# Decoder layer kernel: three elementwise sums moved from GpSimd to VectorE, and two one-column steps written as a tensor with two scalars

## The chip, the cores and the metric

One core of one Trainium2 chip runs the kernel. The metric is the device time of one execution in microseconds (us). A core has TensorE (PE: matmuls and transposes, with its weight loads PEld), VectorE (DVE), ScalarE (ACT), GpSimd (POOL) and SyncE (SP, which here only issues transfers). Each engine has a program of its own, in order, and they meet at semaphores.

## The reference, cut to what matters

One pre-norm decoder layer over 32 sequences of 128 tokens by 512 features: self attention, cross attention to a context of 128 tokens, and a mixture of 64 experts of which every token takes 8.

```python
def _layernorm(x, axis=-1, eps=1e-05):
    m = jnp.mean(x, axis=axis, keepdims=True)
    v = jnp.var(x, axis=axis, keepdims=True)
    return (x - m) / jnp.sqrt(v + eps)
...
    x = x + _L0_attn_ref(_layernorm(x, axis=-1), L0_attn_Wq, L0_attn_bq, L0_attn_Wk, L0_attn_bk, L0_attn_Wv, L0_attn_bv, L0_attn_Wo, L0_attn_bo)
    x = x + _L0_xattn_ref(_layernorm(x, axis=-1), ctx_2048, L0_xattn_wq, L0_xattn_bq, L0_xattn_wkv, L0_xattn_bkv, L0_xattn_wp, L0_xattn_bp)
    x = x + _L0_ffn_ref(_layernorm(x, axis=-1), L0_ffn_router_w, L0_ffn_w_gate, L0_ffn_w_up, L0_ffn_w_down)
    return x
```

Keys and values of the cross attention are projections of the context in full precision. Queries and output of the cross attention are quantised to 8 bits and back.

## The kernel before, in words

A tile is one sequence, 128 tokens on the 128 partitions. The first phase (to about 1240 us) is a software pipeline: in iteration `cur` the engines work at once on five tiles, `cur - 1` (its first layer norm), `cur - 2` (projection of queries and keys), `cur - 3` (self attention, context keys), `cur - 4` (cross attention) and `cur - 5` (second sum, third layer norm, router, scatter of the normed rows to the experts' places in DRAM). There is one `body(cur)` for each engine, a list written out by hand that fixes the order of that engine's steps. Iterations 7 to 32 are a hardware loop, those before and after it are written out. The second phase goes through the 64 experts.

A full-precision projection is made of matmuls on a high part and a low part. For the context, `ctx_hi` (L1747) rounds the loaded `ctx_sb` to `cT_hi`, and `ctx_lo` (L1756) makes the rest, `cT_lo = ctx_sb - cT_hi`. TensorE reads both for the keys (`cross_keys_a`, `cross_keys_c`, `cross_keys_b`) and in the next iteration for the values (`cross_values_b`, `_a`, `_c`).

`bias_residual` (L1768) adds the output bias of the self attention to the residual input `x_res`, which `first_sum` (L1362) adds to the projection one iteration later. `bias_first_sum` (L1775) adds the cross attention's output bias to `x1` and leaves it in `x1_bias` for `second_sum` (L1317, L1320), one iteration later. `ctx_lo`, `bias_residual` and `bias_first_sum` are GpSimd's here, beside `ctx_hi`, the power -1/2 of the three layer norms (`rsqrt`, L1741), `number_tokens` (L1763) and the scatter (L1786, eight indirect DMAs a tile).

The layer norms (kinds "self", "cross", "ffn") go from VectorE (`norm_start`: L1242, L1245, L1247) to GpSimd (`rsqrt`) and back (`norm_scale`: L1252, L1255, L1257, one Newton step on one column). `ffn_shifted` (L1454) makes the shift that ScalarE needs for `ffn_normed` (L1082).

VectorE's part of `body` around the change, in its order (line of the instruction): `cross_max_0`, `cross_max_1` (L1276), `copy_cross_values` (L1437), `ffn_rsqrt` (L1252, L1255, L1257), `ffn_shifted` (L1454), `self_statistics` (L1242, L1245, L1247), `max_3`, `max_1`, `max_2`, `max_0` (L1276), `self_rsqrt`, `norm_probs_3`, `norm_probs_2` (L1282, L1285), `copy_cross_keys` (L1480), `norm_probs_1`. ScalarE's exponentials `exp_3`, `exp_2` and so on (L985) wait for the maxima and are waited for by `norm_probs_3` and `norm_probs_2`. TensorE's `turn_probs_3` (L533) comes right after `logits` (L555) in its order and waits for `copy_cross_keys`:

```python
            def turn_probs_3(m):
                reached(pe, e_xk, m, 1, 1)
                turn_probs(1, 3, p_pT)
```

`until` is a semaphore wait, and `reached` waits for the value that step j of tile m leaves.

Of the kernel before, what the change touches and what calls it, by code (L numbers as in the profile page):

```python
# [38 lines left out]
B = 32  # L39
# [66 lines left out]
def layer(nc, x, ctxT_in, qT_w, kT_w, vT_w, oT_w, xkT_w, xvT_w, xq_w, xp_w, biases, vb, xkb, xvb, ob, xbq, xbp, routerT,  # L106
# [10 lines left out]
    with st:  # L117
# [167 lines left out]
        g_cT = sem("pool_ctxT")  # L285
        g_x1b, g_tok = sem("pool_x1_bias"), sem("pool_token_number")
        g_res = sem("pool_residual_bias")
# [63 lines left out]
        def _(sp):  # L351
# [48 lines left out]
            def load_context(m):  # L400
                reached(sp, g_cT, m - 1, 2, 2)
                sp.dma_start(ctx_sb[:, :].rearrange("p (t n) -> p t n", t=KT),
                             ctxT_in[tile(m)].rearrange("(t p) n -> p t n", p=P)).then_inc(s_ctx, 16)
# [37 lines left out]
            for cur in range(B + 1, B + 6):  # L441
                body(cur)
                if cur == B + 3:
                    for projected in (p_q, p_k, p_v, p_xk, p_o):
                        sp.wait_ge(projected, 3 * B)
                    for k in range(2):
                        load_weights(k, k)
                if cur == B + 4:
                    for k in range(2, 8):
                        load_weights(k, k)  # L450
                    sp.wait_ge(p_xv, 3 * B)
                    for k in range(8, 10):
                        load_weights(k, k)
                    sp.wait_ge(p_xpv, 4 * B)
                    sp.wait_ge(g_res, B)
                    for k in range(10, 14):
                        load_weights(k, k)
# [28 lines left out]
        def _(pe):  # L486
# [151 lines left out]
            def cross_keys_a(m):  # L638
                reached(pe, g_cT, m, 2, 1)
# [12 lines left out]
            def cross_keys_c(m):  # L652
                reached(pe, g_cT, m, 2, 2)
                project(1, cT_hi, cT_lo, "xk", 2, False, False).then_inc(p_xk, 1)
# [583 lines left out]
        def _(dve):  # L1238
# [10 lines left out]
            def norm_scale(kind, m):  # L1249

                s, c = d_ln[kind], ln[kind]
                dve.scalar_tensor_tensor(out=c["t"], in0=c["v"], scalar=c["r0"], in1=c["r0"], op0=ALU.mult,  # L1252
                                         op1=ALU.mult).then_inc(s, 1)
# [105 lines left out]
            def first_sum(m):  # L1359
                reached(dve, p_o, m, 3, 3)  # L1360
                reached(dve, g_x1b, m - 1, 1, 1)
# [39 lines left out]
            def second_sum(m):  # L1401
# [3 lines left out]
                if isinstance(m, int):  # L1405
                    reached(dve, g_x1b, m, 1, 1)
# [32 lines left out]

            def ffn_rsqrt(m):  # L1440
# [11 lines left out]
            def ffn_shifted(m):  # L1452
                reached(dve, d_ln["ffn"], m, 7, 6)
                dve.scalar_tensor_tensor(out=ffn_shift, in0=ln["ffn"]["mv"][:, 0:1], scalar=-1.0, in1=ln["ffn"]["r"],  # L1454
                                         op0=ALU.mult, op1=ALU.mult).then_inc(d_ln["ffn"], 1)
# [75 lines left out]
            def body(cur):  # L1531
# [36 lines left out]
                if has(cur - 4):  # L1568
                    copy_cross_values(cur - 4)
                if has(cur - 5):  # L1570
# [3 lines left out]
                if has(cur - 1):  # L1574
                    self_statistics(cur - 1)
                if has(cur - 3):
# [161 lines left out]
        def _(pool):  # L1738
# [14 lines left out]
            def ctx_lo(m):  # L1753
                reached(pool, g_cT, m, 2, 1)
                reached(pool, p_xv, m - 1, 3, 3)
                pool.tensor_tensor(flat(cT_lo), ctx_sb[:, :], flat(cT_hi).bitcast(F32), ALU.subtract).then_inc(g_cT, 1)  # L1756

# [8 lines left out]
            def bias_residual(m):  # L1766
                reached(pool, s_x_res, m, 16, 16)
                pool.tensor_tensor(x_res[:, :], x_res[:, :], att_bias[:, :], ALU.add).then_inc(g_res, 1)  # L1768

# [3 lines left out]

            def bias_first_sum(m):
                pool.tensor_tensor(x1_bias, x1[:, :], xp_bias[:, :], ALU.add).then_inc(g_x1b, 1)  # L1775
# [14 lines left out]
            def body(cur):  # L1790
# [4 lines left out]
                if has(cur - 3):  # L1795
                    ctx_lo(cur - 3)
                if has(cur - 5):
                    number_tokens(cur - 5)
                if has(cur - 3):
                    bias_residual(cur - 3)  # L1800
                if has(cur - 1):
                    self_power(cur - 1)
                if has(cur - 4):
                    bias_first_sum(cur - 4)
# [113 lines left out]
```

## Time and profile before

| | |
|---|---|
| median of 3 runs | 1647.8 us (1643.46 to 1648.24) |
| the profiled execution | 1644.18 us, of which the span is 1642.4 us |
| mean granted TensorE clock | 0.972 |
| busy share of the span | PE 92%, PEld 71%, DVE 74%, ACT 52%, POOL 42% |
| first phase / second phase | to about 1240 us / 1240 to 1642 us |

Rows of the timeline begin with the start in us from the span's first instruction and the duration in us. "[0.64 <-DVE ...]" is the engine's idle time just before the row and the instruction that ended it. Two VectorE instructions that do not depend on each other overlap by some 0.08 us, so the spacing of their starts is less than the duration. One iteration of the pipeline takes 35.6 us.

### The profile page before, as it was taken

To read this page: it belongs to the slowest core of one execution; us is meant where nothing else is said; L and a number is where in the kernel's file an instruction comes from. 1 tells how busy PE (TensorE), PEld (TensorE's weight loads), DVE (VectorE), ACT (ScalarE), POOL (GpSimd) and SP (SyncE) were. 2 spreads that over 40 slices of the span, in tenths; PEclk is the share of its full clock that TensorE was granted. 3 is DMA by queue.
4 is the path that set the end of the run, shared out by engine and by line. 5 is a ranking of instruction groups with operands and counts; after the bars stand their busy time and mean duration, and the time that the engine had idled before them with its cause. 6 is when DMAs were issued, how large, how long until landed. Compare 5 with 4: busy or idle time off the path is not lost.

```text
span 1642.4 us, 34879 instructions
## 1 busy us (share of the span) xinstructions
PE 1515.1 (92%) x11025; PEld 1158.6 (71%) x11058; DVE 1222.1 (74%) x3203; ACT 853.8 (52%) x2737; POOL 682.9 (42%) x656
## 2 busy tenths in 40 slices
PE   2799999999999999999999999999888888888895
PEld 1577778777778777777877787887645655556563
DVE  6578888889888888888888888888842444444453
ACT  3356666555666655666665566665532333333342
POOL 0013443344443334444334444433443445455465
PEclk9799999999999999999999999999999999999998
DMA  9752322222111101111001011010196999999964
GB/s 323 282 221 84 110 95 89 88 101 107 65 44 30 26 27 31 26 38 32 26 26 32 26 38 32 26 27 21 42 372 207 275 273 275 269 270 284 279 97 51
DMA packets 159883, 195.68 MB, mean 119 GB/s; under 512 B 39686, under 2 KB 122118, under 8 KB 159825
## 3 DMA queue, kind: packets, MB, share of 16 engines
q1 hardware_dynamic: 120912, 157.14, 29.2%
q0 software_dynamic: 38912, 37.87, 11.2%
q8 instruction: 24, 0.39, 0.1%
q14 instruction: 35, 0.28, 0.1%
HBM read 127.47 MB, written 130.29 MB: 157 GB/s over the span
## 4 chain that ended last, share of the span: by engine, by line
PE 61%; DMA 20%; issue 8%; POOL 3%; DVE 1%; ACT 1%; POOLq 0%; SPq 0%; DVEq 0%; ACTq 0%
PE bank L508 30%; DMA out<-x,slots 19%; PE bank L533 7%; PE bank L541 6%; PE bank L490 5%; PE bank L526 4%; PE bank L514 3%; PE bank L549 2%; PE bank L555 2%; PE bank L521 1%; POOL routed L1786 1%; PE bank L495 1%; PE bank L925 0%; ACT probs L985 0%; POOL small L1741 0%
## 5 line engine op out<-in xcount | busy, mean ns | idle before, releaser
L985 ACT ACTIVATE probs<-bank,small 128x128 f32<-128x128 f32 x1024 | 328.0, 417 | 46.0 <-DVE small L1276 46.0
L1786 POOL DMA_INDIRECT routed<-row,slots x248 | 258.7, 1043 | 77.6 <-issue 71.3
L1741 POOL TENSOR_TENSOR small<-small,half 128x1 f32<-128x1 f32 x96 | 62.1, 646 | 540.2 <-DVE small L1247 540.2
L1856 POOL DMA_INDIRECT out<-x,slots x128 | 200.9, 1569 | 197.5 <-DMA out<-x,slots 144.2
L979 ACT ACTIVATE probsT<-bank 128x512 f32<-128x512 f32 x256 | 163.2, 653 | 27.3 <-PE bank L533 27.3
L1276 DVE TENSOR_REDUCE small<-bank 128x4 f32<-128x512 f32 x256 | 161.5, 683 | 12.8 <-PE bank L526 11.6
L533 PE MATMUL bank<-idf,probs 128*128 128x128 f32 x1024 | 154.7, 279 | 3.2 <-DVE xk_sb L1480 2.4
L979 ACT ACTIVATE xo8T<-bank 128x512 bf16<-128x512 bf16 x32 | 19.1, 597 | 241.4 <-PE bank L495 241.4
L1696 DVE TENSOR_SCALAR slots<-pairs 128x1 uint32<-128x1 f32 x128 | 13.7, 149 | 174.0 <-DMA out<-x,slots 170.5
L533 PEld LDWEIGHTS bank<-idf,probs 128*128 128x128 f32 x1024 | 118.7, 143 | 28.7 <-issue 6.1
L985 ACT ACTIVATION_READ_ACCUMULATOR probs<-bank,small 128x1 f32 x512 | 131.7, 257 | 0.0
L541 PE MATMUL bank<-xv,probsT 128*128 128x33 f32 x1024 | 119.8, 272 | 0.0
L541 PEld LDWEIGHTS bank<-xv,probsT 128*128 128x128 f32 x1024 | 119.4, 192 | 0.0
L1205 ACT ACTIVATE xn<-bank 128x192 f32<-128x192 f32 x64 | 21.2, 331 | 153.8 <-PE bank L925 153.8
L925 PE MATMUL bank<-w_gate_up,x_res 128*128 128x384 f32 x256 | 98.9, 535 | 0.0
L925 PE MATMUL bank<-w_gate_up,x_in 128*128 128x384 f32 x256 | 96.3, 523 | 0.6 <-issue 0.6
L1285 DVE TENSOR_TENSOR probs<-probs,small 128x512 f32<-128x512 f32 x128 | 88.6, 693 | 4.4
L925 PEld LDWEIGHTS bank<-w_gate_up,x_res 128*128 128x128 f32 x256 | 51.0, 210 | 30.0 <-issue 8.2
L925 PEld LDWEIGHTS bank<-w_gate_up,x_in 128*128 128x128 f32 x256 | 49.7, 204 | 30.3 <-issue 7.3
L508 PE MATMUL bank<-w_q_hi,xT_hi 128*128 128x512 f32 x128 | 54.7, 427 | 17.4 <-POOL bias_of L1832 17.4
L1747 POOL CAST cT_hi<-ctx_sb 128x512 fp32r<-128x512 f32 x32 | 19.6, 613 | 105.4 <-PE bank L508 57.6
L1024 ACT ACTIVATE wide_b<-bank,xq_bs,xq_ws 128x128 f32<-128x128 f32 x128 | 48.1, 456 | 23.9 <-PE bank L490 23.9
(244 smaller groups left out, 4000.0 us busy)
## 6 DMA issues: line engine op xcount, KB each, us to landing
w_gate_up<-in_w_gate SPq DMA_DIRECT2D x128, 192.0 KB, 3.7
w_gate_up<-in_w_up SPq DMA_DIRECT2D x128, 192.0 KB, 3.9
w_down<-in_w_down SPq DMA_DIRECT2D x128, 192.0 KB, 4.4
routed<-empty_row SPq DMA_DIRECT2D x4, 5120.0 KB, 19.6
x_in<-in_x SPq DMA_DIRECT2D x32, 256.0 KB, 3.1
ctx_sb<-in_ctxT_in SPq DMA_DIRECT2D x32, 256.0 KB, 2.8
x_res<-in_x SPq DMA_DIRECT2D x32, 256.0 KB
out<-x SPq DMA_DIRECT2D x32, 256.0 KB, 2.1
```

What stands on the lines that cost most here:

```text
L490: last = pe.transpose(bank[:, b, t * P:(t + 1) * P], src[:, t * P:(t + 1) * P], idf[:, :])
L508: done = pe.matmul(bank[:, b, :], lhsT, rhs, start=first and k == 0, stop=last and k == len(steps) - 1)
L526: last = pe.matmul(bank[:, b, i * P:(i + 1) * P], q[own, i, :], keys[own, i, :], start=not masked, stop=not masked or i == NG - 1)
L533: last = pe.transpose(bank[:, b, j * P:(j + 1) * P], probs[:, g, j * P:(j + 1) * P], idf[:, :])
L541: last = pe.matmul(bank[:, b, at:at + VW], probsT[:, g, i * P:(i + 1) * P], vals[:, h, :], start=True, stop=True)
L925: last = pe.matmul(bank[:, 2 + k % 2, 0:2 * F], rowsT[k % 2][:, t * P:(t + 1) * P], w_gu[k][:, :, t, :], start=(t == 0), stop=(t == KT - 1))
L979: act.activation(dst, src, ACT.Copy).then_inc(done, 1)
L985: last = act.activation(probs[:, g, j * P:(j + 1) * P], bank[:, b, j * P:(j + 1) * P], ACT.Exp, bias=negated[:, h:h + 1], **({"accum_out": ...
L1276: dve.tensor_reduce(negated[:, g * GH:(g + 1) * GH], bank[:, b, :].rearrange("p (j k) -> p j k", j=GH), AX_X, ALU.max, negate=True).then_i ...
L1285: dve.tensor_tensor(heads, heads, own.unsqueeze(2).to_broadcast([P, GH, P]), ALU.mult).then_inc(d_norm, 1)
L1786: pool.indirect_dma_start(routed, bass.IndirectOffsetOnAxis(ap=slots_of(m)[:, k:k + 1], axis=0), row_of(m)[:, :], None, bounds_check=SLOTS ...
L1856: pool.indirect_dma_start(out.rearrange("b p (h c) -> (b p h) c", h=2), bass.IndirectOffsetOnAxis(ap=place_of[k % 2][:, half_:half_ + 1], ...
```

## The change

`ctx_lo`, `bias_residual` and `bias_first_sum` become VectorE's, at three places of its order: `ctx_lo` behind `copy_cross_values`, `bias_residual` and `bias_first_sum` between `self_statistics` and `max_3`. Semaphores follow: `first_sum` waits for one more. The first step of `norm_scale` and `ffn_shifted`, each a scalar_tensor_tensor on one column, become tensor_scalar with two scalars.

```diff
@@ norm_scale
-                dve.scalar_tensor_tensor(out=c["t"], in0=c["v"], scalar=c["r0"], in1=c["r0"], op0=ALU.mult,
-                                         op1=ALU.mult).then_inc(s, 1)
+                dve.tensor_scalar(c["t"], c["v"], c["r0"], c["r0"], ALU.mult, ALU.mult).then_inc(s, 1)
@@ load_context (SP), cross_keys_a, cross_keys_c (PE)
-                reached(sp, g_cT, m - 1, 2, 2)
+                reached(sp, d_cT, m - 1, 1, 1)
...
-                reached(pe, g_cT, m, 2, 1)
+                reached(pe, g_cT, m, 1, 1)
...
-                reached(pe, g_cT, m, 2, 2)
+                reached(pe, d_cT, m, 1, 1)
@@ first_sum
-                reached(dve, g_x1b, m - 1, 1, 1)
+                reached(dve, d_x1b, m - 1, 1, 1)
+                reached(dve, d_res, m, 1, 1)
@@ VectorE, new steps
+            def ctx_lo(m):
+                reached(dve, g_cT, m, 1, 1)
+                dve.tensor_tensor(flat(cT_lo), ctx_sb[:, :], flat(cT_hi).bitcast(F32), ALU.subtract).then_inc(d_cT, 1)
+
+            def bias_residual(m):
+                reached(dve, s_x_res, m, 16, 16)
+                dve.tensor_tensor(x_res[:, :], x_res[:, :], att_bias[:, :], ALU.add).then_inc(d_res, 1)
+
+            def bias_first_sum(m):
+                dve.tensor_tensor(x1_bias, x1[:, :], xp_bias[:, :], ALU.add).then_inc(d_x1b, 1)
@@ ffn_shifted
-                dve.scalar_tensor_tensor(out=ffn_shift, in0=ln["ffn"]["mv"][:, 0:1], scalar=-1.0, in1=ln["ffn"]["r"],
-                                         op0=ALU.mult, op1=ALU.mult).then_inc(d_ln["ffn"], 1)
+                dve.tensor_scalar(ffn_shift, ln["ffn"]["mv"][:, 0:1], ln["ffn"]["r"], -1.0, ALU.mult,
+                                  ALU.mult).then_inc(d_ln["ffn"], 1)
@@ VectorE's body
                 if has(cur - 4):
                     copy_cross_values(cur - 4)
+                if has(cur - 3):
+                    ctx_lo(cur - 3)
...
                 if has(cur - 1):
                     self_statistics(cur - 1)
+                if has(cur - 3):
+                    bias_residual(cur - 3)
+                if has(cur - 4):
+                    bias_first_sum(cur - 4)
                 if has(cur - 3):
                     max_3(cur - 3)
@@ GpSimd's body: the three steps are gone
```

## Rows read from the trace of the kernel before

**Rows 1.** One stretch: its length, then busy us of PE, PEld, DVE, ACT, POOL:
```profile
600.00:635.60 35.60, 35.46 (x288) 28.27 (x289) 31.65 (x83) 21.88 (x77) 15.02 (x17) 1.00 0.10 30
```

**Rows 2.** Timeline of DVE, from the cross values' copy to the first maximum:
```profile
629.66 0.68 DVE L1437 TENSOR_TENSOR xv<-bank,xv_bias 128x512 f32<-128x512 f32 x1
630.26 0.91 DVE L1252 SCALAR_TENSOR_TENSOR small<-small 128x1 f32<-128x1 f32 x1
...
631.58 1.19 DVE L1454 SCALAR_TENSOR_TENSOR small<-small 128x1 f32<-128x1 f32 x1
632.69 0.68 DVE L1242 BATCH_NORM_STATS2 small<-x_in 128x6 f32<-128x512 f32 x1
...
633.79 2.48 DVE L1276 TENSOR_REDUCE small<-bank 128x4 f32<-128x512 f32 x4
```

**Rows 3.** Timeline of POOL, same stretch:
```profile
629.88 1.26 POOL L1756 TENSOR_TENSOR cT_lo<-ctx_sb,cT_hi 128x512 fp32r<-128x512 f32 x1
...
631.49 1.26 POOL L1768 TENSOR_TENSOR x_res<-x_res,att_bias 128x512 f32<-128x512 f32 x1
633.93 0.57 POOL L1741 TENSOR_TENSOR small<-small,half 128x1 f32<-128x1 f32 x1 [1.18 <-DVE small L1247]
```

**Rows 4.** Timeline of ACT, the start of the self attention's exponentials:
```profile
634.52 0.37 ACT L985 ACTIVATE probs<-bank,small 128x128 f32<-128x128 f32 x1 [0.64 <-DVE small L1276]
```

**Rows 5.** Timeline of DVE, `norm_probs_2` and `copy_cross_keys` (35.6 us before: same place):
```profile
602.33 0.18 DVE L1282 RECIPROCAL small<-small 128x4 f32<-128x4 f32 x1 [0.30 <-ACT probs L985]
602.54 0.69 DVE L1285 TENSOR_TENSOR probs<-probs,small 128x512 f32<-128x512 f32 x1
603.15 0.68 DVE L1480 COPY xk_sb<-bank 128x512 f32<-128x512 f32 x1
```

**Rows 6.** Timeline of PE, around `turn_probs_3`, mid-loop:
```profile
602.90 1.08 PE L555 MATMUL bank<-router_w,x3T 128*128 128x64 f32 x8
603.89 1.09 PE L533 MATMUL bank<-idf,probs 128*128 128x128 f32 x8
```

**Rows 7.** Timeline of PE, the same place in iteration 35:
```profile
1175.06 1.08 PE L555 MATMUL bank<-router_w,x3T 128*128 128x64 f32 x8
1175.98 1.04 PE L533 MATMUL bank<-idf,probs 128*128 128x128 f32 x8
```

**Rows 8.** Timeline of DVE, the iteration of one late scatter:
```profile
665.24 0.68 DVE L1437 TENSOR_TENSOR xv<-bank,xv_bias 128x512 f32<-128x512 f32 x1
...
667.74 1.39 DVE L1257 TENSOR_TENSOR small<-small 128x1 f32<-128x1 f32 x1
...
670.38 2.48 DVE L1276 TENSOR_REDUCE small<-bank 128x4 f32<-128x512 f32 x4
```

**Rows 9.** Timeline of PE, `turn_probs_3` two iterations after that of rows 6:
```profile
676.08 1.09 PE L533 MATMUL bank<-idf,probs 128*128 128x128 f32 x8
```

**Rows 10.** Timeline of DVE, iteration 35:
```profile
1164.26 0.69 DVE L1437 TENSOR_TENSOR xv<-bank,xv_bias 128x512 f32<-128x512 f32 x1 [0.29 <-PE bank L508]
...
1169.58 2.48 DVE L1276 TENSOR_REDUCE small<-bank 128x4 f32<-128x512 f32 x4
```

**Rows 11.** Groups of DVE's instructions by line (busy us, mean ns | idle before):
```profile
L1262 DVE TENSOR_SCALAR xn<-x_in,small 128x512 f32<-128x512 f32 x32 | 17.2, 538 | 0.1
L1371 DVE TENSOR_SCALAR xo_tmp<-xatt,small 128x512 f32<-128x512 f32 x32 | 15.3, 479 | 0.0
L1334 DVE TENSOR_SCALAR small<-small 128x1 f32<-128x1 f32 x32 | 6.9, 215 | 1.1
```

**Rows 12.** Timeline of DVE, the first two iterations of self attention:
```profile
60.82 2.09 DVE L1313 TENSOR_TENSOR roped<-roped,wide_a 128x1024 f32<-128x1024 f32 x1
...
99.79 2.48 DVE L1276 TENSOR_REDUCE small<-bank 128x4 f32<-128x512 f32 x4 [0.67 <-PE bank L526]
```

**Rows 13.** Timeline of DVE and then POOL, during the cross norm's power:
```profile
615.88 0.43 DVE L1375 TENSOR_SCALAR xo<-xo_tmp 128x512 bf16<-128x512 f32 x1
...
615.53 0.82 POOL L1741 TENSOR_TENSOR small<-small,half 128x1 f32<-128x1 f32 x1 [15.38 <-DVE small L1247]
```

More of the change, by code:

```diff
@@ L284, in layer @@
         g_pow = {k: sem(f"pool_rsqrt_{k}") for k in ln}
-        g_cT = sem("pool_ctxT")
-        g_x1b, g_tok = sem("pool_x1_bias"), sem("pool_token_number")
-        g_res = sem("pool_residual_bias")
+        g_cT, d_cT = sem("pool_ctxT_hi"), sem("dve_ctxT_lo")
+        g_tok = sem("pool_token_number")
+        d_x1b, d_res = sem("dve_x1_bias"), sem("dve_residual_bias")
         s_vspread, s_att = sem("value_bias_spread"), sem("attention_bias")
@@ L454, in _ @@
                     sp.wait_ge(p_xpv, 4 * B)
-                    sp.wait_ge(g_res, B)
+                    sp.wait_ge(d_res, B)
                     for k in range(10, 14):
@@ L1405, in second_sum @@
                 if isinstance(m, int):
-                    reached(dve, g_x1b, m, 1, 1)
+                    reached(dve, d_x1b, m, 1, 1)
                 second_sum_of(6, m)
@@ L1751, in ffn_power @@
                 rsqrt("ffn")
[L1753 to L1756, printed above, removed]
             def number_tokens(m):
@@ L1764, in number_tokens @@
                                    ALU.add).then_inc(g_tok, 1)
-            def bias_residual(m):
-                reached(pool, s_x_res, m, 16, 16)
-                pool.tensor_tensor(x_res[:, :], x_res[:, :], att_bias[:, :], ALU.add).then_inc(g_res, 1)
             def self_power(m):
@@ L1772, in self_power @@
                 rsqrt("self")
-            def bias_first_sum(m):
-                pool.tensor_tensor(x1_bias, x1[:, :], xp_bias[:, :], ALU.add).then_inc(g_x1b, 1)
             def cross_power(m):
@@ L1794, in body @@
                     ffn_power(cur - 5)
-                if has(cur - 3):
-                    ctx_lo(cur - 3)
                 if has(cur - 5):
                     number_tokens(cur - 5)
-                if has(cur - 3):
-                    bias_residual(cur - 3)
                 if has(cur - 1):
                     self_power(cur - 1)
-                if has(cur - 4):
-                    bias_first_sum(cur - 4)
                 if has(cur - 3):
```

## The prediction

> **What bounds the kernel now.** I read the stretches view first, then the timelines of the engines over one iteration, then the waits. In a mid-loop iteration of 35.60 us TensorE is busy for 35.46, VectorE for 31.65 and GpSimd for 15.02 [rows 1]. That looks like a kernel bound by TensorE, in which VectorE has 4 us to spare. A busy TensorE can still be held for less than the overlap of its instructions, so I followed who hands work to whom.
>
> Follow one chain. `copy_cross_values` starts at 629.66, and from there VectorE works without a wait up to `max_3` at 633.79, which is 4.13 us later [rows 2]. ScalarE has idled for 0.64 us until that maximum ends, and starts the exponentials at 634.52 [rows 4]. It then works through its list at its own pace; the reader sees in the same place one iteration earlier that VectorE's `norm_probs_2` idles 0.30 us for it, and that `copy_cross_keys` follows and ends at 603.15 + 0.68 = 603.83 [rows 5]. TensorE's `turn_probs_3`, which needs this copy, starts at 603.89 [rows 6]. So the last link is 0.06 us wide. In iteration 35, where nothing holds it there, `turn_probs_3` starts 0.92 us after `logits`; mid-loop it is 0.99 [rows 6, 7]. TensorE is held for 0.07 us an iteration by a chain that runs through VectorE's stretch of 4.13 us. Idle time of VectorE elsewhere is no help: it lies behind waits for ScalarE.
>
> The trace holds its own test of this. Once, GpSimd's scatter is late, and VectorE's stretch lasts 670.38 - 665.24 = 5.14 us, 1.01 more [rows 8]. `turn_probs_3` then starts at 676.08, 72.19 us after 603.89, which is two iterations of 35.60 and 0.99 more [rows 6, 9]. A microsecond in this stretch is a microsecond of the kernel. The change edits exactly this stretch.
>
> **The change, part by part.** Removed, stalls: in the stretch VectorE's two one-column scalar_tensor_tensor wait behind GpSimd. L1252 starts at 630.26 and ends at 631.17, L1756 of GpSimd ends at 631.14; L1454 starts at 631.58 and ends at 632.77, L1768 ends at 632.75 [rows 2, 3]. Both GpSimd instructions leave, so the stalls do.
>
> What the two instructions cost without a stall is not in the trace in their new form. A one-column tensor_scalar with one scalar from memory and one constant takes 0.215 us; a second scalar from memory adds 0.538 - 0.479 = 0.06 on 512 columns [rows 11]. So the first becomes 0.27, plus 0.03 to the dependent next one: 0.30. Bounds: 0.24, if the second scalar is free, and 0.36, if it costs twice that. It was 0.91 + 0.03 = 0.94. The shift becomes 0.215, and the independent next one overlaps it by 0.08: 0.13, where it was 632.69 - 631.58 = 1.11 [rows 2]. Removed: 0.64 + 0.98 = 1.62 us a tile.
>
> Added: three tensor_tensor of 512 columns with both inputs in SBUF. The one in rows 5 takes 0.69 and the next starts 603.15 - 602.54 = 0.61 after it. All three are independent of their neighbours: 1.83 us a tile, each in the stretch. They wait for nothing: `cT_hi` is ready ahead of 629.88, since GpSimd makes it before L1756 [rows 3], and `ctx_lo` would start at 630.26. `x_res` is loaded half an iteration before. `load_context` on SP now waits for an end at about 630.95 in place of 631.14 [rows 3], nothing is behind it that is urgent.
>
> Sum of the stretch: 4.13 - 1.62 + 1.83 = 4.34 us, so +0.21 a tile, between +0.15 and +0.27. What is late next is ScalarE's `exp_3`, then `norm_probs_2`, `copy_cross_keys` and TensorE, all by the same 0.21, as in the late iteration. The stretch is filled like this in iterations 6 to 33; 27 of them are regular: 27 x 0.21 = +5.7 us.
>
> One iteration has the late scatter: 5.14 becomes 4.34, since the freed GpSimd is no longer in the way: -0.8. Iteration 35 has a second one, 1169.58 - 1164.26 = 5.32 us [rows 10]. It has no `self_statistics` any more, which takes 633.79 - 632.69 = 1.10 [rows 2], so it becomes 4.34 - 1.10 = 3.24: -2.1, of which I take -2.0.
>
> The start: at 60.82 the rotation of the first tile takes 2.09 behind GpSimd [rows 12]. With 512 columns at 0.69 [rows 5] 1024 take at most 1.38, so at least 0.7 goes: I take -0.8. In the next iteration there is no stalled instruction to relieve, and the three additions meet an idle time of 0.67 [rows 12]: 1.83 - 0.67 = +1.16. Together +0.36.
>
> Two small ones have no row. `first_sum` gets a third wait, for a value long reached, and the cross norm's step gets the second scalar, both on the way from the output projection to `turn_quantised_x`. At nothing they cost 0, at 0.06 a tile over 31 tiles 1.9 us; I take 0.5, since TensorE's order has some play there. The self norm's step grows too, under the 0.30 us that VectorE waits for ScalarE [rows 5]; without that cover it would be another 0.06 a tile, 1.6 us. The second phase has none of the moved work: 0.
>
> Sum: 5.7 - 0.8 - 2.0 + 0.4 + 0.5 = +3.8 us. The profiled execution becomes 1644.18 + 3.8 = 1648.0. The median shown is 3.6 us above that execution, so the median becomes 1647.8 + 3.8 = **1651.6 us** (+0.23%).
>
> **The rivals.** *A. The stretch grows by 0.21* (forecast): 1651.6, by its bounds and 1 us for the start 1649 to 1655.
>
> *B. A new stall behind the power.* After `self_statistics` GpSimd starts the self norm's power, 0.57 us [rows 3], while VectorE runs `bias_residual` and then wants `bias_first_sum`. If the power gets in between and keeps VectorE out, it costs up to 0.57 a tile: 27 x 0.57 = 15.4, so 1667.0. For it: a tensor_tensor of VectorE does stall behind GpSimd, L1257 took 1.39 [rows 8]. Against it: the cross norm's power is stretched to 0.82 by VectorE's tensor_scalars, and the tensor_scalar L1375 that starts within it at 615.88 takes a plain 0.43 [rows 13]; a power seems to hold VectorE off for next to nothing. It decides only if the power takes the port in the gap and holds it over 0.04 us.
>
> The Trainium skill, "SBUF — State Buffer", section "Who interferes with whom", says of exactly these pairs that a VectorE instruction with two SBUF inputs and a GpSimd instruction that reads SBUF share a port pair, which whoever issues first keeps for its whole instruction. By that rule the power would hold off `bias_first_sum` for its whole 0.57 us, and the sum would be B's. On the long GpSimd instructions the trace agrees (0.91 and 1.19 us where the stalls end with them, [rows 2, 3]); on the power the row speaks against it [rows 13].
>
> *C. The stretch is not the bound after all.* If ScalarE or TensorE has play that the rows don't show, the 0.21 vanish and only gains stay: -0.8 at the start, -1.0 and -2.0 at the late scatters, 1647.8 - 3.8 = 1644.0. For it: TensorE is held for 0.07 us only. Against it: the 0.99 of rows 9.
>
> *D. The chain gets shorter*, the one on the faster side: if the three additions cost under 0.5 each where they stand, the stretch shrinks by more than 0.07, TensorE is no longer held, and 27 x 0.07 = 1.9 come on top of C's: 1642.1. Against it: the 0.61 between starts in rows 5, on the same form of instruction.
>
> *E. More late scatters in plain runs.* Each is worth 1.0 to the change. The runs lie 4.8 us apart; four more would give 1647.6, nine more would be needed for a clear gain.
>
> *F. The cross norm's way is as tight* as the other and its two small costs come to 0.1 a tile: 31 x 0.1 = 3.1 in place of 0.5, 1654.2.
>
> **How the numbers follow.** Chances: A 0.55, B 0.12, C 0.13, D 0.08, E 0.05, F 0.07. A measurement of this kernel tells about 0.3% from no change, 4.9 us: faster below 1642.9, slower above 1652.7. A lies 1.1 us under that line, so of its 0.55 I put 0.33 within and 0.22 above. Slower: 0.22 + 0.12 + 0.07 = 0.41. Faster: D and some of E, 0.10. Within: 0.49. The range leaves out B and most of D: from a little under C, 1643, to 1658, which takes in F and a B of a third of its price. A's own is 1649 to 1655.
>
> **What would show it.** In the changed profile: the first step of the ffn norm at about 0.27 us and the shift at 0.21, neither stalled (if stalled, something else of GpSimd reads there); `ctx_lo`, `bias_residual`, `bias_first_sum` at 0.69 each (over 0.75 for the last is B); from `copy_cross_values` to `max_3` 4.34 us (4.1 or less is D); starts of `turn_probs_3` 35.8 us apart (35.6 with a stretch of 4.34 is C); no iteration of 36.6. The prediction is wrong if the two rewritten steps cost far more than 0.3, if waits for reached values cost time on VectorE, or if the end of iteration 35 does not carry through to the second phase.

## The result and the profile after

The changed kernel takes 1649.18 us against 1643.62 us for the kernel before (medians of 17 runs each); the ratio is 1.0031, with an interval from 1.0019 to 1.0044. One execution of the changed kernel, 17% longer at a lower clock, is left out of the ratio. The profiled execution of after took 1648.34 us with a span of 1646.5 us, against 1644.18 and 1642.4 before.

The first table of the page of after, busy us, share of the span and instructions of each engine:

```profile
PE 1515.3 (92%) x11025; PEld 1157.2 (70%) x11058; DVE 1230.3 (75%) x3299; ACT 854.5 (52%) x2737; POOL 574.9 (35%) x560
```

GpSimd has 108 us less to do, VectorE 8 us more, and TensorE the same. The stretch of one mid-loop iteration, to be held against [rows 1]:

```profile
600.00:635.83 35.83, 35.69 (x289) 28.29 (x289) 31.92 (x85) 21.90 (x76) 11.71 (x13) 1.00 0.09 29
```

The iteration is 35.83 us long, 0.23 more. The timeline of VectorE from the cross values' copy to the first maximum, which answers to [rows 2]:

```profile
637.35 0.68 DVE L1437 TENSOR_TENSOR xv<-bank,xv_bias 128x512 f32<-128x512 f32 x1
637.95 0.68 DVE L1442 TENSOR_TENSOR cT_lo<-ctx_sb,cT_hi 128x512 fp32r<-128x512 f32 x1
638.54 0.27 DVE L1252 TENSOR_SCALAR small<-small 128x1 f32<-128x1 f32 x1
...
639.23 0.21 DVE L1465 TENSOR_SCALAR small<-small 128x1 f32<-128x1 f32 x1
639.36 0.68 DVE L1242 BATCH_NORM_STATS2 small<-x_in 128x6 f32<-128x512 f32 x1
...
640.47 0.69 DVE L1446 TENSOR_TENSOR x_res<-x_res,att_bias 128x512 f32<-128x512 f32 x1
641.08 0.69 DVE L1449 TENSOR_TENSOR wide_a<-x,xp_bias 128x512 f32<-128x512 f32 x1
641.68 2.48 DVE L1275 TENSOR_REDUCE small<-bank 128x4 f32<-128x512 f32 x4
```

The stretch is 641.68 - 637.35 = 4.33 us, where 4.34 was forecast. The two rewritten steps take 0.27 and 0.21, the step behind each of the three additions starts 0.59 to 0.61 later, and nothing is stalled. TensorE from the step ahead of `logits` to `turn_probs_3`, which answers to [rows 6]:

```profile
608.68 1.87 PE L541 MATMUL bank<-xv,probsT 128*128 128x33 f32 x16
610.52 1.10 PE L555 MATMUL bank<-router_w,x3T 128*128 128x64 f32 x8
611.57 1.09 PE L533 MATMUL bank<-idf,probs 128*128 128x128 f32 x8
```

It starts 1.05 us after `logits`; before it was 0.99, and 0.92 where nothing holds it [rows 6, 7]. That is only 0.06 of the 0.23. More of it lies one step earlier. `logits` itself starts 610.52 - 608.68 = 1.84 us after the step ahead of it, where it was 602.90 - 601.19 = 1.71:

```profile
601.19 1.87 PE L541 MATMUL bank<-xv,probsT 128*128 128x33 f32 x16
```

`logits` needs `x3T`, which ScalarE makes (L979). Here are the timelines of ScalarE, before and then after:

```profile
637.75 0.64 ACT L979 ACTIVATE x3T<-bank 128x512 f32<-128x512 f32 x1
...
645.63 0.64 ACT L979 ACTIVATE x3T<-bank 128x512 f32<-128x512 f32 x1
```

In both kernels this comes 3.23 us after the first exponential (634.52 before, 642.40 after), so a later maximum makes `x3T` later by the same amount. A third part, 0.03, stands at `turn_quantised_x`, which starts 0.68 us after the step ahead of it in place of 0.65. Together that is 0.06 + 0.13 + 0.03 = 0.22 of the 0.23.

**Where the time went.** The stores of x2 mark the end of each tile's attention. In the timelines of SyncE they come as follows. The first is at 126.32 before and at 130.66 after (+4.34). From there to the last but one, at 1193.17 and 1201.03, it is another +3.52. From that store to the end of the span it is 449.2 and 445.5 (-3.8). The very last store is no such mark, since it stands in SyncE's order behind the loads of the second phase's weights, as in after:

```profile
1237.17 0.91 SPq L345 DMA_DIRECT2D w_down<-in_w_down  x2
1238.12 0.44 SPq L393 DMA_DIRECT2D out<-x  x1
```

The part behind the last but one store varies from 445 to 459 us among before, after and experiments 1 to 4 and 6 to 8, whose code for the second phase is the same, so it says nothing of the change. Two parts are left: a loss of 4.3 us in the first 130 us, and one of 3.5 us in the loop. Together they are 7.9 us in these two executions, where the medians of all executions differ by 5.6; what makes up the difference between the two isn't shown.

The loop's part goes as forecast. The intervals between stores grow from 35.60 to 35.83. The one with the late scatter was 36.58 and is 35.84 (-0.74; forecast -0.8). The one that holds iteration 35 goes from 33.60 to 31.65 (-1.95; forecast -2.0), and TensorE's timeline carries this gain to the last tile: its step at 1222.81 before (L490) comes at 1230.66 after, 7.85 later, as it is at iteration 35. The other 28 intervals gain 3.52 + 0.74 + 1.95 = 6.2 us, where 5.7 + 0.5 were forecast.

The start's part does not. The stretches view of TensorE's clock shows it (columns as in [rows 1]; the third from the right is the granted clock). Before:

```profile
100.00:105.00 5.00, 5.00 (x36) 4.37 (x33) 4.29 (x12) 4.74 (x25) 1.66 (x2) 1.00 1.01 388
105.00:110.00 5.00, 4.88 (x49) 4.40 (x49) 3.88 (x11) 4.00 (x17) 0.00 (x0) 1.00 1.03 403
```

After:

```profile
100.00:105.00 5.00, 4.46 (x33) 3.95 (x30) 4.58 (x12) 4.59 (x25) 0.00 (x0) 1.00 1.02 395
105.00:110.00 5.00, 4.61 (x23) 4.61 (x23) 2.91 (x8) 3.16 (x13) 0.00 (x0) 0.54 1.03 396
110.00:115.00 5.00, 5.00 (x43) 3.88 (x47) 0.63 (x2) 2.15 (x6) 0.00 (x0) 0.50 0.66 251
```

In the second iteration of self attention TensorE is busy for 4.46 of 5 us where it was busy for 5.00, and then its granted clock goes from 1.00 (2.4 GHz) to 0.50 (1.2 GHz) for some 10 us. The timeline of TensorE shows one `turn_probs` in that time at nearly twice its length, behind `copy_cross_keys`. Before and after:

```profile
105.73 1.09 PE L533 MATMUL bank<-idf,probs 128*128 128x128 f32 x8
...
105.39 1.97 PE L533 MATMUL bank<-idf,probs 128*128 128x128 f32 x8 [0.93 <-DVE xk_sb L1491]
```

Up to here after was not late at all, but 0.34 us early. The whole loss of 4.3 us in the first store comes behind this step, with the clock down.

### The profile page after: what moved, and what is told of

Read it like the earlier page. It is cut to its first block, busy times and chain, and to the rows that moved or that the text cites. A ratio compares the mean times of both kernels' runs of the same rounds, so it can differ in the third digit from the quotient of the medians.

```text
span 1646.5 us, 34797 instructions
## 1 busy us (share of the span) xinstructions
PE 1515.3 (92%) x11025; PEld 1157.2 (70%) x11058; DVE 1230.3 (75%) x3299; ACT 854.5 (52%) x2737; POOL 574.9 (35%) x560
## 4 chain that ended last, share of the span: by engine, by line
PE 64%; DMA 19%; issue 7%; DVE 2%; POOL 1%; ACT 1%; POOLq 0%; SPq 0%; DVEq 0%
PE bank L508 31%; DMA out<-x,slots 19%; PE bank L533 7%; PE bank L541 6%; PE bank L490 5%; PE bank L526 4%; PE bank L514 3%; PE bank L549 2%; PE bank L555 2%; PE bank L521 1%; PE bank L495 1%; POOL routed L1791 1%; ACT probs L985 0%; PE bank L925 0%; DVE small L1275 0%
## 5 line engine op out<-in xcount | busy, mean ns | idle before, releaser
L1758 POOL TENSOR_TENSOR small<-small,half 128x1 f32<-128x1 f32 x96 | 74.4, 775 | 652.8 <-DVE small L1247 652.8
L979 ACT ACTIVATE probsT<-bank 128x512 f32<-128x512 f32 x256 | 162.9, 652 | 29.7 <-PE bank L533 29.5
L533 PE MATMUL bank<-idf,probs 128*128 128x128 f32 x1024 | 156.1, 281 | 4.1 <-DVE xk_sb L1491 3.4
L979 ACT ACTIVATE xo8T<-bank 128x512 bf16<-128x512 bf16 x32 | 19.1, 597 | 241.6 <-PE bank L495 241.6
L533 PEld LDWEIGHTS bank<-idf,probs 128*128 128x128 f32 x1024 | 119.7, 144 | 30.6 <-issue 6.3
L925 PE MATMUL bank<-w_gate_up,x_res 128*128 128x384 f32 x256 | 94.4, 515 | 0.0
L925 PE MATMUL bank<-w_gate_up,x_in 128*128 128x384 f32 x256 | 91.9, 504 | 0.5 <-issue 0.5
L1024 ACT ACTIVATE wide_b<-bank,xq_bs,xq_ws 128x128 f32<-128x128 f32 x128 | 48.1, 457 | 23.9 <-PE bank L490 23.9
L508 PE MATMUL bank<-w_o_hi,attT_hi 128*128 128x512 f32 x132 | 56.0, 424 | 1.7 <-issue 0.9
```

The source lines that it names most:

```text
L508: done = pe.matmul(bank[:, b, :], lhsT, rhs, start=first and k == 0, stop=last and k == len(steps) - 1)
L533: last = pe.transpose(bank[:, b, j * P:(j + 1) * P], probs[:, g, j * P:(j + 1) * P], idf[:, :])
L925: last = pe.matmul(bank[:, 2 + k % 2, 0:2 * F], rowsT[k % 2][:, t * P:(t + 1) * P], w_gu[k][:, :, t, :], start=(t == 0), stop=(t == KT - 1))
L979: act.activation(dst, src, ACT.Copy).then_inc(done, 1)
L1758: pool.tensor_tensor(c["r0"], c["v"], half[:, :], ALU.pow).then_inc(g_pow[kind], 1)
```

## The experiments

Each is read against runs of the kernel before that were made together with it. "Stretch" is the time from `copy_cross_values` to `max_3`, and "period" the usual time between two stores of x2.

**1. The two bias steps out of the stretch.** In after, the same instructions at a place where VectorE has waited for ScalarE:

```diff
-                if has(cur - 3):
-                    bias_residual(cur - 3)
-                if has(cur - 4):
-                    bias_first_sum(cur - 4)
                 if has(cur - 3):
                     max_3(cur - 3)
...
+                if has(cur - 3):
+                    bias_residual(cur - 3)
+                if has(cur - 4):
+                    bias_first_sum(cur - 4)
                 if has(cur - 3):
                     att_lo(cur - 3)
```

> The changed kernel, with bias_residual and bias_first_sum moved out of VectorE's stretch between copy_cross_values and max_3 and placed right ahead of att_lo, where VectorE idles 0.93 us for ScalarE. Same work, same engine, another place. Theory 1 (the length of the stretch sets the period, a tile for a tile): stretch 4.33 - 2 x 0.61 = 3.1 us, turn_probs_3 no longer held, period 35.5 to 35.6 in place of 35.83, so about 27 x 0.3 = 7 us less than the changed kernel, ratio to the kernel before 0.996 to 0.999. Theory 2 (VectorE's added load of 1.8 us a tile costs wherever it stands, for instance through the port it shares with GpSimd): period stays at 35.8, ratio 1.003. Theory 3 (the 4 us later start in the profile of the changed kernel come from a fall of TensorE's clock at 105 to 116 us, brought on by the longer hold in the second iteration): the hold at turn_probs_3 there shrinks from 0.93 to near nothing, and the clock stays at 1.0 there.

Measured: 1640.6 us, ratio to before 0.9958 (0.9945 to 0.9971). The timeline of VectorE of this kernel gives a stretch of 3.11 us:

```profile
627.68 0.68 DVE L1437 TENSOR_TENSOR xv<-bank,xv_bias 128x512 f32<-128x512 f32 x1
...
630.79 2.48 DVE L1275 TENSOR_REDUCE small<-bank 128x4 f32<-128x512 f32 x4
```

and that of TensorE shows `turn_probs_3` no longer held, 0.92 us behind `logits`:

```profile
636.52 1.08 PE L555 MATMUL bank<-router_w,x3T 128*128 128x64 f32 x8
637.44 1.04 PE L533 MATMUL bank<-idf,probs 128*128 128x128 f32 x8
```

The period is 35.52, the first store comes at 125.37, and the clock from 100 to 115 us is 1.00. The work is the same as in after, and only its place differs: the loss of after is that of the stretch, not of VectorE's busy time. With the longer stretch gone, `logits` is free too: it starts 1.70 us after the step ahead of it.

**2. The old forms with the moved work.** After, with both tensor_scalar back as scalar_tensor_tensor:

```diff
-                dve.tensor_scalar(c["t"], c["v"], c["r0"], c["r0"], ALU.mult, ALU.mult).then_inc(s, 1)
+                dve.scalar_tensor_tensor(out=c["t"], in0=c["v"], scalar=c["r0"], in1=c["r0"], op0=ALU.mult,
+                                         op1=ALU.mult).then_inc(s, 1)
...
-                dve.tensor_scalar(ffn_shift, ln["ffn"]["mv"][:, 0:1], ln["ffn"]["r"], -1.0, ALU.mult,
-                                  ALU.mult).then_inc(d_ln["ffn"], 1)
+                dve.scalar_tensor_tensor(out=ffn_shift, in0=ln["ffn"]["mv"][:, 0:1], scalar=-1.0, in1=ln["ffn"]["r"],
+                                         op0=ALU.mult, op1=ALU.mult).then_inc(d_ln["ffn"], 1)
```

> The changed kernel with its two one-column tensor_scalar turned back to scalar_tensor_tensor (the three sums stay on VectorE). Theory 1: no long GpSimd instruction is left in the stretch, so they do not stall any more in either form, and the old form is shorter (0.21 against 0.27, 0.16 against 0.21): stretch 4.33 - 0.11 = 4.22, period 35.72, 3 us less than the changed kernel, ratio to before about 1.001. Theory 2 (the new form is what took the stalls away): L1252 of the ffn norm and the shift stall again, at 0.4 us or more, behind the power or number_tokens, and the period is 36.0 or more, ratio 1.006.

Measured: 1649.62 us, ratio 1.0020 (1.0007 to 1.0032). The timeline of VectorE:

```profile
637.57 0.21 DVE L1252 SCALAR_TENSOR_TENSOR small<-small 128x1 f32<-128x1 f32 x1
...
638.20 0.16 DVE L1466 SCALAR_TENSOR_TENSOR small<-small 128x1 f32<-128x1 f32 x1
```

With GpSimd's long instructions gone the old forms don't stall, and they are shorter than the new ones: 0.21 against 0.27, and 0.16 against 0.21. The stretch is 4.26, the period 35.77, and the clock falls at the start as in after (first store 130.38). So the two halves of the change are two cures for one stall, and whoever moves the work away has no use for the new forms. (The ratios of this kernel and of after, 1.0020 and 1.0031, are too close to tell apart; the 0.06 us of the period are read from the traces.)

**3. The new forms alone.** Before, with only those lines changed the other way round; GpSimd keeps its three steps.

```diff
-                dve.scalar_tensor_tensor(out=c["t"], in0=c["v"], scalar=c["r0"], in1=c["r0"], op0=ALU.mult,
-                                         op1=ALU.mult).then_inc(s, 1)
+                dve.tensor_scalar(c["t"], c["v"], c["r0"], c["r0"], ALU.mult, ALU.mult).then_inc(s, 1)
...
-                dve.scalar_tensor_tensor(out=ffn_shift, in0=ln["ffn"]["mv"][:, 0:1], scalar=-1.0, in1=ln["ffn"]["r"],
-                                         op0=ALU.mult, op1=ALU.mult).then_inc(d_ln["ffn"], 1)
+                dve.tensor_scalar(ffn_shift, ln["ffn"]["mv"][:, 0:1], ln["ffn"]["r"], -1.0, ALU.mult,
+                                  ALU.mult).then_inc(d_ln["ffn"], 1)
```

> The kernel before with only the two one-column steps turned to tensor_scalar; the three sums stay on GpSimd. Theory 1 (scalars from memory do not come through the port shared with GpSimd): neither step stalls, 0.27 and 0.21 us in place of 0.91 and 1.19; the one-column tensor_tensor between them may stall by some 0.4 us until ctx_lo of GpSimd ends. Stretch 2.7 to 2.9 us in place of 4.13, turn_probs_3 not held, no late iteration: period 35.5, ratio 0.996 to 0.998. Theory 2 (the stall moves on to the next instruction of VectorE that needs the port, and all of it stays): stretch near 4.1, period 35.6, ratio 1.000. Theory 3 (the tensor_scalar stalls like the old form): the same numbers as before plus 0.1 a tile.

Measured: 1640.75 us, ratio 0.9964 (0.9952 to 0.9977). The timeline of VectorE (here L1257 of before is L1256):

```profile
628.88 0.26 DVE L1252 TENSOR_SCALAR small<-small 128x1 f32<-128x1 f32 x1
629.18 0.15 DVE L1254 TENSOR_SCALAR small<-small 128x1 f32<-128x1 f32 x1
629.37 0.42 DVE L1256 TENSOR_TENSOR small<-small 128x1 f32<-128x1 f32 x1
629.83 0.21 DVE L1453 TENSOR_SCALAR small<-small 128x1 f32<-128x1 f32 x1
```

The tensor_scalars take 0.26 and 0.21 beside a GpSimd that works; the tensor_tensor between them is stalled to 0.42 and ends at 629.79, when GpSimd's `ctx_lo` ends (629.77). The stretch is 2.77 us, the period 35.47, and no iteration is late. This edit, two lines of the whole, brings as much as the whole change does with its steps at their best place (0.9958 in experiment 1). The kernel with the old forms and the steps at that place was not run.

**4. After once more,** a look for the clock.

> The changed kernel once more, for its start and its second phase. Theory 1 (the clock's fall at 105 to 116 us follows from the longer hold of TensorE in the second iteration): the fall is there again, at the same place, and the first store of x2 is issued near 130.7 us. Theory 2 (chance): the clock stays up, the first store comes near 126.5 us. The period is 35.83 by either, and the second phase varies by several us either way.

Measured: 1655.3 us in one run. The first store is at 130.32, the granted clock 0.53 and 0.50 in the stretches from 105 to 115 us, the period 35.84. The fall comes again, at the same place.

**5. A fourth addition in the stretch.** After, with one more 512-column tensor_tensor ahead of `bias_first_sum`; it writes into scratch space, and its result is not used.

```diff
+            def repeat_sum(m):
+                dve.tensor_tensor(xq_tmp, x1[:, :], xp_bias[:, :], ALU.add)
...
+                if has(cur - 4):
+                    repeat_sum(cur - 4)
                 if has(cur - 4):
                     bias_first_sum(cur - 4)
```

> The changed kernel with one more tensor_tensor of the same form and size (the first sum's bias once more, into a scratch tile) inside VectorE's stretch, between bias_residual and bias_first_sum. Theory 1 (every us of the stretch is a us of the period): stretch 4.33 + 0.61 = 4.94 us, period 35.83 + 0.60 = 36.4, about 28 x 0.6 = 17 us more than the changed kernel, ratio to the kernel before 1.013. Theory 2 (TensorE is the bound and the handover at turn_probs_3 has play left): less than 0.3 a tile, ratio under 1.009.

Measured: 1784.76 us, ratio 1.0846 (1.0824 to 1.0868). The stretch came out as forecast, 4.94 us. The period is 41.0 and not the 36.4 or so that 0.61 would give; all theories missed this. The stretches view of this kernel, which repeats every 41 us:

```profile
600.00:605.00 5.00, 5.00 (x38) 3.93 (x41) 1.28 (x7) 1.59 (x4) 0.00 (x0) 0.50 0.00 0
...
630.00:635.00 5.00, 4.91 (x34) 4.18 (x32) 4.65 (x11) 3.56 (x19) 0.18 (x1) 1.00 0.00 0
635.00:640.00 5.00, 4.60 (x25) 4.49 (x25) 4.30 (x12) 4.79 (x22) 0.00 (x0) 0.59 0.00 0
640.00:645.00 5.00, 5.00 (x30) 4.29 (x30) 2.15 (x13) 1.18 (x3) 0.00 (x0) 0.50 0.00 0
```

and its timeline of TensorE:

```profile
635.52 1.69 PE L555 MATMUL bank<-router_w,x3T 128*128 128x64 f32 x8 [0.40 <-ACT x3T L979]
637.01 1.91 PE L533 MATMUL bank<-idf,probs 128*128 128x128 f32 x8
638.71 3.46 PE L541 MATMUL bank<-xv,probsT 128*128 128x33 f32 x16
```

An idle time of 0.40 us opens ahead of `logits`, which waits for ScalarE's `x3T`, and about there the granted clock goes from 1.00 to 0.50 and stays down for some 10 us in this and nearly every iteration (only two intervals of the loop are shorter, 37.97 and 36.43). Over the 45 us around this place TensorE is busy for 44.5.

**6. The same addition outside the stretch,** ahead of `att_lo`:

```diff
+                if has(cur - 4):
+                    repeat_sum(cur - 4)
                 if has(cur - 3):
                     att_lo(cur - 3)
```

> The same extra tensor_tensor, but placed right ahead of att_lo, where VectorE of the changed kernel idles 0.93 us. Theory 1: it disappears in the wait: period 35.83, ratio 1.003 as for the changed kernel. Theory 2 (VectorE's load counts wherever it stands): period 36.4, ratio 1.013.

Measured: 1650.11 us, ratio 1.0021 (1.0003 to 1.0039), period 35.83: the same as after. The clock falls at the start as in after. The instruction that costs 135 us at one place costs nothing at another.

**7. Only the start relieved.** After, with the two bias steps ahead of `att_lo` for iterations up to 6, and in the stretch for the rest:

```diff
-                if has(cur - 3):
-                    bias_residual(cur - 3)
-                if has(cur - 4):
-                    bias_first_sum(cur - 4)
+                if not (isinstance(cur, int) and cur <= 6):
+                    if has(cur - 3):
+                        bias_residual(cur - 3)
+                    if has(cur - 4):
+                        bias_first_sum(cur - 4)
...
+                if isinstance(cur, int) and cur <= 6:
+                    if has(cur - 3):
+                        bias_residual(cur - 3)
+                    if has(cur - 4):
+                        bias_first_sum(cur - 4)
```

> The changed kernel, with bias_residual and bias_first_sum ahead of att_lo in the written-out iterations up to 6 alone; from iteration 7 on they stand in the stretch as in the change. Theory 1 (the hold of TensorE at turn_probs_3 in the second iteration brings the clock's fall, and that costs 4 us): no fall at 105 to 116 us, the first store of x2 near 125.4 us in place of 130.7, the period 35.83 as before, 5 us less than the changed kernel, ratio to before 1.000. Theory 2 (the fall has another cause, for instance less GpSimd work): the fall stays, first store at 130 us, ratio 1.003.

Measured: 1645.37 us, ratio 1.0009 (0.9996 to 1.0022). The first store comes at 125.03, the clock stays at 1.00, and the period is 35.85. The start's part of the loss is gone (5.6 us in the first store, 1.0031 - 1.0009 = 0.0022 or 3.6 us in the time, though the intervals of the two ratios overlap slightly) and the loop's is there as before. GpSimd has the same little work here as in after, so it is the place of the two steps in the first iterations that brings the fall.

**8. One of the two bias steps out.** After, with only `bias_first_sum` ahead of `att_lo`:

```diff
-                if has(cur - 4):
-                    bias_first_sum(cur - 4)
                 if has(cur - 3):
                     max_3(cur - 3)
...
+                if has(cur - 4):
+                    bias_first_sum(cur - 4)
                 if has(cur - 3):
                     att_lo(cur - 3)
```

> The changed kernel with bias_first_sum alone moved ahead of att_lo; bias_residual stays in the stretch. Stretch 4.33 - 0.61 = 3.72 us. Theory 1 (the stretch binds only above about 4.06 us, the length at which TensorE is no longer held): period as for both moved out, 35.52, ratio 0.996 to 0.998; in the second iteration the hold is 0.6 us shorter, the clock may stay up or not. Theory 2 (the gain is proportional to what is taken out): period half way, 35.67.

Measured: 1637.04 us, ratio 0.9961 (0.9946 to 0.9975); stretch 3.73, period 35.51. Taking the second step out too (experiment 1) brings nothing more in the period.

**9 to 11. In a slower setting.** The last three were made together at a time when the kernel before took 1755.16 us, and have periods of 38 to 44 us. The record gives them the chip number of experiments 5 to 8, where the same kernel took 1644.25; whether it was the same chip is not known. The waits view of these traces has ScalarE's L1024 and VectorE's L1411 wait for something that it puts on no engine of the core: 56 to 63 and 79 to 82 us in all from 170 to 1290 us, and 0 in experiment 1. What that is I can't tell. The three are compared only with the kernel before as it ran beside them. After itself was not run there.

Experiment 9 is after with the waits of `first_sum` in another order, so that the one which comes last is asked last:

```diff
             def first_sum(m):
-                reached(dve, p_o, m, 3, 3)
                 reached(dve, d_x1b, m - 1, 1, 1)
                 reached(dve, d_res, m, 1, 1)
+                reached(dve, p_o, m, 3, 3)
```

> The changed kernel with the three waits of first_sum in another order: the two on VectorE's own old results first, the one on TensorE's output projection last. In the traces first_sum starts 0.63 us after the start of the projection's last matmul where it has the third wait, and 0.53 us where it has two. Theory 1 (each wait that stands behind the one that is released last costs some 0.1 us, and turn_quantised_x is tight, so the change pays it in each tile): first_sum starts 0.45 to 0.53 us after that matmul, and the period falls by what TensorE is held at turn_quantised_x, 35.83 to about 35.78; ratio to the changed kernel 0.999. Theory 2 (the 0.1 us is not the waits' order): start after 0.63 us still, period 35.83.

Measured: 1768.17 us, ratio 1.0082 (1.0047 to 1.0116). Without a run of after beside it, this ratio says nothing of the order; the start of `first_sum` does, and is read below. Experiment 10 is the kernel of experiment 1 with the same reordering.

> Both steps moved ahead of att_lo (as in e_out) and first_sum's waits in the order of e_order. Theory 1: period 35.52 falls to 35.42 to 35.47, since now only TensorE's own handovers are left: 2 to 3 us less than e_out, ratio to the kernel before 0.994 to 0.996. Theory 2 (the order is worth nothing): 35.52, 0.996.

Measured: 1747.18 us, ratio 0.9959 (0.9926 to 0.9993); without the reordering it was 0.9958. The timelines of VectorE and TensorE show `first_sum` and the last matmul of the output projection, first in after:

```profile
621.31 0.69 DVE L1362 TENSOR_TENSOR x<-bank,x_res 128x512 f32<-128x512 f32 x1 [0.52 <-PE bank L508]
...
620.68 0.40 PE L508 MATMUL bank<-w_o_lo,attT_hi 128*128 128x512 f32 x1
```

then in experiment 10:

```profile
616.28 0.69 DVE L1362 TENSOR_TENSOR x<-bank,x_res 128x512 f32<-128x512 f32 x1 [0.53 <-PE bank L508]
...
615.65 0.40 PE L508 MATMUL bank<-w_o_lo,attT_hi 128*128 128x512 f32 x1
```

From start to start it is 0.63 in both, and 0.64 in experiment 9. Before it is 613.55 - 613.02 = 0.53, and 0.53 in experiment 3, which have two waits. So the kernels with a third wait have 0.10 us more, wherever the one that comes last stands. The order of the waits, which I took for the cause, is not it. That it is the third wait itself is the likely reading; no run takes it away alone.

Experiment 11 is after with a 256-column addition in the stretch, half of experiment 5:

```diff
+            def repeat_sum(m):
+                dve.tensor_tensor(xq_tmp[:, 0:HALF], x1[:, 0:HALF], xp_bias[:, 0:HALF], ALU.add)
...
+                if has(cur - 4):
+                    repeat_sum(cur - 4)
                 if has(cur - 4):
                     bias_first_sum(cur - 4)
```

> The changed kernel with half of e_rep_in's extra work in the stretch: a tensor_tensor of 256 columns, about 0.34 us from start to start, stretch 4.67 us. e_rep_in showed a period of 41.0 us, not 36.4, with TensorE's clock at 0.5 for a part of each iteration. Theory 1 (a cliff: the clock falls once TensorE's idle in the stretch of 5 us around turn_probs_3 is long enough, and the half dose is below it): period 35.83 + 0.34 = 36.17, clock 1.0, ratio 1.010. Theory 2 (the half dose is over the edge too): period near 40.7, ratio 1.08.

Measured: 1791.32 us, ratio 1.0194 (1.0141 to 1.0247), 1.1% above experiment 9 by the two ratios. By their ratios theory 1 had some 0.7% there and theory 2 some 7.7%, so it is nearer the first; but the clock does not stay at 1.00, as the first had it. Its mean clock is 0.941 against 0.961. At the start the clock falls as in after in this one and in experiment 9 (0.50 to 0.55 in the stretch from 110 to 115 us), and stays at 1.00 in experiment 10. In the loop it falls in some iterations (0.63 and 0.50 from 640 to 650 us, behind an idle time of 0.40 us ahead of `logits` at 639.88) and not in others (1.00 from 680 to 695 us, behind the same 0.40 at 683.75). So the length of that idle time alone does not decide. Experiment 9 has falls in its loop too (0.69 from 645 to 650 us). The periods vary too much to read a slope.

## Where the prediction held and where it failed, step by step

The forecast was 1651.6 us, from 1643 to 1658, and the median is 1649.18. As a difference it was +3.8 us (+0.23%) and is +5.6 between the medians (+0.31% by the ratio): the level came out lower because the kernel before measured 1643.6 over more runs, where 1647.8 was shown. The result lies on the line that was drawn at 0.3%, and I gave "within" 0.49 and "above" 0.41. That the time came out so near 1651.6 is in part luck: the lower level of the kernel before took off 4.2 us, and the loss at the start, which the sum did not have, added to it.

**The stretch as the bound** (rival C denied): right. Put in a row, all runs but experiments 9 to 11 give the curve that the prediction had one slope of:

| kernel | stretch, us | period, us |
|---|---|---|
| new forms alone | 2.77 | 35.47 |
| both bias steps out | 3.11 | 35.52 |
| one bias step out | 3.73 | 35.51 |
| before | 4.13 | 35.60 |
| after, old forms | 4.26 | 35.77 |
| after | 4.33 | 35.83 |
| a fourth addition | 4.94 | 41.0 |

Up to 3.73 us the stretch is free. From 4.13 to 4.33 it costs 0.23 us for 0.20. Beyond, TensorE's clock comes in. The prediction placed the kernel before at the very edge, "held for 0.07 us", and the other side of the edge is worth just that: 35.60 - 35.51 = 0.09. The path was right up to ScalarE's exponentials, and named one of two ends. Most of the 0.23 (0.13) comes through `x3T` and `logits`, and only 0.06 through `norm_probs_2`, `copy_cross_keys` and `turn_probs_3`, the one end that the prediction followed. The sum came out right, since both hang on the same exponentials.

**The terms of the stretch**: the sum is right to 0.01, each term to 0.03. The new forms cost 0.27 and 0.21 (forecast 0.27 and 0.215), the additions 1.80 (1.83).

**The two late iterations**: right, -0.74 and -1.95.

**The wait of `first_sum`**: right in size. I took 0.5 us for it and the second scalar together. `first_sum` does start 0.10 us later, but TensorE's `turn_quantised_x`, which lies behind it, comes only 0.03 later (0.68 in place of 0.65; 0.65 too in experiment 3, 0.66 to 0.70 in the kernels with the third wait). Over 28 iterations that is 0.8 us. It agrees with the periods of the kernels that have the third wait, after and the one with the old forms: they stand 0.03 and 0.04 us above what a slope of 1 from 4.13 us gives.

**The start**: this step failed. The prediction took -0.8 for the first iteration and 1.83 - 0.67 = +1.16 for the next, together +0.36. The stalled rotation at 60.82 is 0.87 shorter, and the second iteration's TensorE steps come 1.14 us earlier (the L533 at 97.08 comes at 95.94). The additions then take back only 0.80 of it, as `turn_probs_3` starts 0.34 earlier. So in waits alone the start would have been a gain of 0.3. What the sum left out is the clock. TensorE, now ahead of VectorE's chain, idled for 0.93 us at `turn_probs_3`, its clock fell to 1.2 GHz, and the first store came 4.3 us late in place of 0.4. The fall thus costs some 4.7 us. Experiments 1, 7 and 8, in which the two steps or one of them are elsewhere at that time, have no fall, and the first store at 125.4, 125.0 and 123.0; experiments 2 and 4 repeat the fall. That the place of the two steps brings the fall is shown by them. That it goes by way of TensorE's idle time isn't tried by itself, but at this place all traces agree with it: in those with the fall (after and experiments 2, 4, 5, 6, 9 and 11) the row of this `turn_probs_3` has an idle time of 0.89 to 1.45 us, in experiment 8 it has 0.30, and in before and experiments 1, 7 and 10 it has none. So the price of a delay was counted in microseconds of waiting alone, in a stretch where half the clock was at stake.

The Trainium skill, "TensorE: Matmul & The Clock Gate", section "The HAM clock gate (the "warmup" mystery)", describes such a gate with the levels 1.2 and 2.4 GHz. The trace agrees: 0.50 and 1.00 are granted here, one half and the whole.

**Rival B**: refuted. The row that the prediction held against it [rows 13] was no test, since L1375 is a tensor_scalar, which doesn't stall in the new forms either; the changed kernel has the very pair. GpSimd's power of the self norm does overlap `bias_residual`, in the timeline of GpSimd:

```profile
604.79 0.99 POOL L1758 TENSOR_TENSOR small<-small,half 128x1 f32<-128x1 f32 x1 [2.63 <-DVE small L1247]
```

It is the power that gets longer, from 0.57 to 0.99 us, behind `bias_residual` (604.66 to 605.35 on VectorE). `bias_first_sum` starts at 605.27, within the power, and takes a plain 0.68. Over the kernel the groups of VectorE show no stall of any of the three additions:

```profile
L1446 DVE TENSOR_TENSOR x_res<-x_res,att_bias 128x512 f32<-128x512 f32 x32 | 22.1, 691 | 0.0
L1442 DVE TENSOR_TENSOR cT_lo<-ctx_sb,cT_hi 128x512 fp32r<-128x512 f32 x32 | 21.9, 685 | 0.0
L1449 DVE TENSOR_TENSOR wide_a<-x,xp_bias 128x512 f32<-128x512 f32 x32 | 21.9, 684 | 0.0
```

The rule of the Trainium skill, "SBUF — State Buffer", section "Who interferes with whom", that whoever issues first keeps the shared ports for the whole instruction, would, as the prediction read it, have stalled `bias_first_sum` for the power's whole length; the trace does not agree for this pair. That the other one of such a pair has to wait, it does show, at the power, which began within `bias_residual`.

**D, E and F**: the additions did not overlap more than the row said (D). The late scatter came again, at 664.02 and 1166.27 (656.05 and 1156.45 before), and cost nothing any more; there were no more of them than before (E, for this execution). F had the mechanism, but at the end of the way it comes to 0.03 us a tile and not 0.1.

## What to carry to other kernels

Work moved between engines is priced by the place where it lands in the other engine's order. Beside the same new forms, the same three instructions made this kernel 0.3% slower in one place and 0.4% faster in another, and one more of them at the first place cost 8%. Before moving work to cure a stall behind a shared resource, try another form of the stalled instruction that doesn't stall there: here two lines brought as much (0.9964) as the moved work did at its best place (0.9958). And where a delay reaches TensorE, read the granted clock beside the wait, since the loss can be many times the wait: in experiment 5 an idle time of 0.40 us went with a period 41.0 - 35.83 - 0.61 = 4.6 us longer than the addition itself explains.

## What the runs showed of the hardware that was not expected

- A TensorE that is busy for some 99% of the time (44.5 of 45 us in experiment 5) dropped to half its clock behind an idle time of 0.40 us, and did so in nearly each iteration: 41.0 us in place of 35.83 for 0.61 us more on VectorE. The same idle time in experiment 11 brought a fall in one iteration and none in another. At 4.33 us of stretch, in after, the mid-loop period stayed at 35.83, and only the start had a fall.
- `first_sum` on VectorE, with a third semaphore to wait for, long reached, starts 0.10 us later than with two (0.63 against 0.53 after the start of the matmul that releases it), in either order of the waits. No run takes the third wait away alone.
- One-column steps on VectorE: tensor_scalar with two scalars from memory 0.27 us, with one 0.21; scalar_tensor_tensor, unstalled, 0.21 and 0.16. The latter and a tensor_tensor of one column wait behind GpSimd's 512-column instructions (up to 1.19 in [rows 2], 0.42 in experiment 3), the tensor_scalar does not.
- GpSimd's one-column power is stretched beside a tensor_tensor of VectorE (0.57 to 0.99 us), and the next tensor_tensor, which starts within it, takes a plain 0.68.
